# Announcing the closing branch of every tile loop in a four-layer graph network

## The reference

```python
x = _layernorm(x + _L0_gnn_ref(x, edge_index, ...))       # attention over edges, 8 heads, q.k logits, gelu
x = _layernorm(x + _L1_gnn_ref(x, src, dst, edge_type, edge_weight1, bases, w_comp))   # 32 relations of 8 bases
x = _layernorm(x + _L2_gnn_ref(x, src, dst, ...))         # two graph attention layers, 8 heads and 1 head
x = _layernorm(x + _L3_gnn_ref(x, edge_index, ...))       # attention, a state-space scan over sorted nodes, feed-forward
```

## Time and profile before

| | us |
|---|---|
| median of 3 runs | 10471.25 |
| lowest and highest run | 10463.4, 10483.5 |
| the profiled execution | 10561.48 |
| its span, first to last instruction | 10559.3 |
| slot build and first products, about 640 to 1060 | 420 |
| conv, 1060 to 2900 | 1840 |
| relation layer, 2900 to 4545 | 1645 |
| gat1 and gat2, 4545 to 7700 | 3155 |
| last layer, 7700 to 10020 | 2320 |
| join, 10020 to the end | 539 |

### The profile page before, as it was taken

How to read it: one execution, slowest core, us unless ns; L and a number is a source line. 1 busy time by engine, 2 the same in 40 slices (tenths; PEclk the granted TensorE clock), 3 DMA queues, 4 the chain that set the end, 5 groups by cost and what they waited for, 6 DMA issues and landing times. The chain is left out here.

```text
span 10559.3 us, 93192 instructions
## 1 busy us (share of the span) xinstructions
PE 3592.6 (34%) x15280; PEld 2794.6 (26%) x15281; DVE 5663.9 (54%) x11971; ACT 1229.9 (12%) x2744; POOL 5135.2 (49%) x4985
## 2 busy tenths in 40 slices
PE   3034343333255556611122200000034444444434
PEld 3011232222255556510111100000023333333323
DVE  8632666666521111157666656666655555555644
ACT  0001011111100001100000000000011222222211
POOL 0021555555465556656666556666544454444410
PEclk6556666666677778855555555555567666767666
DMA  0111444444222222223323222223222222222200
GB/s 19 51 42 27 120 128 121 120 128 122 77 76 73 65 66 81 67 58 80 80 76 82 60 64 76 75 74 80 62 68 69 78 79 68 76 73 70 60 28 7
DMA packets 485741, 772.46 MB, mean 73 GB/s; under 512 B 296031, under 2 KB 316310, under 8 KB 481979
## 3 DMA queue, kind: packets, MB, share of 16 engines
q0 software_dynamic: 265504, 666.90, 22.9%
q10 hardware_dynamic: 19838, 70.21, 1.8%
q1 hardware_dynamic: 200345, 34.81, 1.8%
HBM read 822.37 MB, written 46.03 MB: 82 GB/s over the span
## 5 line engine op out<-in xcount | busy, mean ns | idle before, releaser
L782 POOL DMA_INDIRECT gat_rows<-scratch_gat,gat_index x1856 | 1861.3, 1003 | 1050.0 <-issue 606.6
L1644 POOL DMA_INDIRECT m_rows<-scratch_gat,m_index x928 | 1064.4, 1147 | 1228.6 <-DVE m_work L1933 893.0
L782 POOL DMA_INDIRECT conv_rows<-scratch_kv,conv_index x928 | 931.4, 1004 | 796.3 <-DVE conv_work L861 363.7
L1211 POOL DMA_INDIRECT rel_rows<-scratch_x,rel_index x928 | 926.5, 998 | 612.5 <-issue 409.3
L1067 PE MATMUL conv_ps<-conv_work,k_ident 128*128 128x256 f32 x1856 | 672.2, 540 | 1275.0 <-DVE conv_work L861 1078.5
L1067 PEld LDWEIGHTS conv_ps<-conv_work,k_ident 128*128 128x128 f32 x1856 | 514.2, 284 | 1433.5 <-DVE conv_work L861 1111.8
L552 PE MATMUL gat_ps<-k_ident,gat_cur 128*128 128x128 f32 x100 | 34.4, 448 | 2350.1 <-issue 1029.4
L871 DVE TENSOR_REDUCE gat_red<-gat_work 128x256 f32<-128x2048 f32 x232 | 832.5, 3589 | 0.0
L1697 PE MATMUL m_ps<-m_work,k_ident 128*128 128x256 f32 x1664 | 556.9, 510 | 702.8 <-DVE m_work L1933 643.6
L1697 PEld LDWEIGHTS m_ps<-m_work,k_ident 128*128 128x128 f32 x1664 | 433.2, 266 | 824.2 <-issue 735.6
L552 PEld LDWEIGHTS gat_ps<-k_ident,gat_cur 128*128 128x128 f32 x100 | 14.5, 204 | 2385.3 <-issue 1045.3
(11 more groups left out here) (449 smaller groups left out, 7916.9 us busy)
## 6 DMA issues: line engine op xcount, KB each, us to landing
m_bc<-scratch_bc ACTq DMA_DIRECT2D x25, 2048.0 KB
gat_rows<-scratch_gat,gat_index POOLq DMA_INDIRECT x1856
conv_rows<-scratch_kv,conv_index POOLq DMA_INDIRECT x928
rel_rows<-scratch_x,rel_index POOLq DMA_INDIRECT x928
m_rows<-scratch_gat,m_index POOLq DMA_INDIRECT x928
scratch_runs<-e_runs_sb SPq DMA_DIRECT2D x1, 12890.6 KB
scratch_kv<-p_row ACTq DMA_DIRECT2D x25, 256.0 KB
gat_index<-scratch_slots SPq DMA_DIRECT2D x232, 4.0 KB
```

The source lines that it names most:

```text
L782: pool.indirect_dma_start(out=rows[b][:, s, :], out_offset=None, in_=table, in_offset=bass.IndirectOffsetOnAxis(ap=index[b][:, s:s + 1], a ...
L1211: pool.indirect_dma_start(out=rows[b][:, g, :], out_offset=None, in_=dr["x1"], in_offset=bass.IndirectOffsetOnAxis(ap=index[b][:, g:g + 1] ...
L1644: pool.indirect_dma_start(out=rows[b][:, s, :], out_offset=None, in_=dr["gat3"], in_offset=bass.IndirectOffsetOnAxis(ap=index[b][:, s:s + ...
```

## The change

A helper `tile_loop` is added, and every loop over tiles, on all five engines and in all stages that have one, is opened with it in place of `eng.Fori`; SP's loop over records in the relation layer too. The inner loops over chunks stay as they are.

```diff
+def tile_loop(nc, eng, first, end):
+
+    return nc.Fori(first, end, engines=(eng.engine,), hint_back_edge=True)
...
-            with v.Fori(0, T) as t:
+            with tile_loop(nc, v, 0, T) as t:
...
-            with sp.Fori(0, T) as t:
+            with tile_loop(nc, sp, 0, T) as t:
                 visit(sp, kp, t, load_record)
...
-            with pool.Fori(1, T) as t:
+            with tile_loop(nc, pool, 1, T) as t:
                 visit(pool, kp, t, gather)
...
-            with sp.Fori(1, last + 1) as r:
+            with tile_loop(nc, sp, 1, last + 1) as r:
                 sp.wait_ge(record_taken, r)
...
-            with eng.Fori(0, T - 2) as t:
+            with tile_loop(nc, eng, 0, T - 2) as t:
                 tile(t, True, True)
...
-            with v.Fori(0, T // B) as i:
+            with tile_loop(nc, v, 0, T // B) as i:
                 st = Steps(v, sems["steps"], BEFORE + i * PER)
```

More of the change, by code:

```diff
@@ L476, in _ @@
             nc.gpsimd.iota(slot_i[:], [[1, RUN]], base=0, channel_multiplier=0).then_inc(sems["zero"], 1)
-            with pool.Fori(0, T) as t:
+            with tile_loop(nc, pool, 0, T) as t:
                 lo, hi = bounds(pool, kp, t)
@@ L506, in _ @@
             pe.wait_ge(sems["loaded"], 16 * LOADS)
-            with pe.Fori(0, T) as t:
+            with tile_loop(nc, pe, 0, T) as t:
                 for k in range(2):
@@ L529, in _ @@
             act.wait_ge(sems["loaded"], 16 * LOADS)
-            with act.Fori(0, T) as t:
+            with tile_loop(nc, act, 0, T) as t:
                 for k in range(2):
@@ L988, in _ @@
             tile(0, True)
-            with v.Fori(1, T) as t:
+            with tile_loop(nc, v, 1, T) as t:
                 tile(t, False)
@@ L1050, in _ @@
             visit(act, kp, 0, exp)
-            with act.Fori(1, T) as t:
+            with tile_loop(nc, act, 1, T) as t:
                 visit(act, kp, t, exp, first_pair(t - 1))
@@ L1097, in _ @@
                 visit(pe, kp, 0, sum_slots)
-                with pe.Fori(1, T) as t:
+                with tile_loop(nc, pe, 1, T) as t:
                     visit(pe, kp, t, sum_slots, first_pair(t - 1))
@@ L2012, in _ @@
             tile(0, True, True, None)
-            with v.Fori(1, T - 2) as t:
+            with tile_loop(nc, v, 1, T - 2) as t:
                 tile(t, True, True, t - 1)
@@ L2073, in _ @@
             prime(pool, dr, spare, sems["written"])
-            with pool.Fori(0, T // B) as i:
+            with tile_loop(nc, pool, 0, T // B) as i:
                 pool.wait_ge(sems["out_ready"], i + 1)
@@ L2096, in turn @@
                 ins.then_inc(sems["turned"], 1)
-            with pe.Fori(0, T // B) as i:
+            with tile_loop(nc, pe, 0, T // B) as i:
                 pe.wait_ge(sems["turn"], i * 3 + 1)
@@ L2143, in take_root @@
                 act.activation(root[:], var[:], ACT.Sqrt).then_inc(sems["root"], 1)
-            with act.Fori(0, T // B) as i:
+            with tile_loop(nc, act, 0, T // B) as i:
                 act.wait_ge(sems["elu_in"], i + 1)
```

## The result

The changed kernel took 10490.32 us (median of 12 runs, 10453.28 to 10505.58), the kernel before beside it 10464.51 us (12 runs, 10439.14 to 10483.5): a ratio of 1.0019, 95% interval 1.0010 to 1.0028. By the ratio that is 20 us more, 10 to 29 by the interval; the two medians stand 26 us apart. The profiled execution of the changed kernel had a span of 10503.8 us in a run of 10505.58; that of the kernel before had been 10559.3 us, in a run of 10561.48. So the two profiled executions stand the other way round than the medians. From here on totals are compared by medians, and only parts by traces.

What follows compares the result with a forecast made beforehand. No engine was taken as the bound; tile heads stand in the chain. Nothing saved, 15 us of added instructions, two thirds showing as 10 us on the 10471.25 us median: 10481 us, range 10440 to 10525.

Steps and rivals of the forecast that it cites:

- the 0.2%: Whole kernel: about 0.2% (21 us) is what a measurement can tell from no change; chance of landing within it 0.67.
- What bounds the kernel: All tile loops: no engine is busy even 55% of the span; the head of a tile stands in the chain.
- Saved term nought: Back edges of all tile loops: none fetches code, so the announcement saves 0 us.
- The fifth rival: DVE's last-layer and PE's relation-layer bodies fetch after all, at most 97 us hidden: 10384 us, chance 0.02.
- Price of the instruction: Tile heads: 0.1 us per announcement (0.02 to 0.3), 148 times, 15 us; ends 3 and 44 us.
- The third rival: Closing branch: the announcement removes the gap to the next instruction, 148 x 0.25 = 37 us back: 10444 us, chance 0.06.
- What covers it: Tile heads: engines not added up, part given back from buffers ahead, two thirds of 15 us shows: 10 us.
- The second rival: Long tile heads: one more 0.7 us sequencer step in 33 heads, 23 us besides the 15: 10509 us, chance 0.10.
- The fetching rival: Tile heads: each announcement fetches its target although present, 148 x 2.1 = 311 us: 10782 us, chance 0.08.

Runs made afterwards that it cites:

- e9_sem8_again: Eight semaphore additions on which nobody waits at every tile head on every engine, no announcement, against the kernel before: 10774.44 us, ratio 1.0204.
- e3_hint8_dve: Eight announcements and a register move at each tile head on DVE alone, none on other engines, against the kernel before: 9237.75 us, ratio 1.0082.
- e4_hint8_rest: Eight announcements and a register move at tile heads on POOL, SP, ACT and PE, none on DVE, against the kernel before: 9178.75 us, ratio 1.0019.
- e5_hint1_all: The changed kernel unaltered, once more beside the kernel before on a chip with long steps: 10603.04 us, ratio 1.0039.
- e8_four_loads_hint: Four value loads per tile head in place of six, plus one announcement on every engine, against the kernel before: 10481.82 us, ratio 0.9918.
- e7_four_loads: Four value loads per tile head in place of six, the other two values summed, no announcement, against the kernel before: 10452.38 us, ratio 0.9893.
- e10_sem8_hint: Eight semaphore additions at every tile head plus one announcement on every engine, against the kernel before: 10844.71 us, ratio 1.0271.
- e12_three_loads: Three value loads per tile head in place of six, with one more schedule row, no announcement, against the kernel before: 10414.13 us, ratio 0.9862.
- e2_nop8_all: Eight no-operations intended, but only one register move added at nearly every tile head on all engines, no announcement, against the kernel before: 9167.62 us, ratio 1.0009.
- the first four runs: Eight announcements on all engines, on DVE alone, on the others alone, and one register move; the kernel before took 9160.75 us on their chip.
- e11_sem7: Seven semaphore additions at every tile head on every engine, no announcement, against the kernel before: 10735.72 us, ratio 1.0167.

## Why the prediction was right, and where its steps were off

**The total.** 20 us slower was measured (10 to 29; 26 by the medians), 10 were forecast, on a base that agrees (10464.51 against 10471.25). The ratio of 1.0019 lies inside the 0.2%, so it came out as forecast, but near the edge, and on a second chip the same kernel was 0.39% slower, outside it. The sign held both times; the size measured was twice and four times the forecast's. On the chip without long steps an announcement comes to 11 us (89/8), almost the 10 of the forecast, but that is partly luck. The price of 0.1 us was too high for it (0.065 to 0.07), and the two thirds that show, on one engine's head alone, were too low. The two errors cancel.

**What bounds the kernel: right.** That the tile's head is in the chain was the base of it all. Eight announcements and a move on DVE alone bring 77 of their 89 us; fewer value loads bring 109 and 151 us.

**Saved term nought: right.** No back edge fetches anything in the kernel before, and no fetch was saved: the stretch without instruction packets stays so. The fifth rival, that the longest bodies fetch after all, was wrong for this placement of the code. What it speaks of happens all the same. With the body starting 40 instructions further on and eight longer (e9_sem8_again), q14 moved five 8 KB packets per iteration (85 in 17) and DVE's back edge took 4 us; no run shows why there and not before. The forecast rested on a margin that it had not measured. And that an announced branch has nothing to save where nothing is fetched was the author's assumption, which no run shows; at the branch itself the runs showed some 0.05 us saved (next paragraph).

**Price of the instruction: a third too high on DVE.** It was 0.1 us by the nearest row; measured are 0.06 in the slot build, 0.065 from eight of them, and 0.08 from an announcement's start to the next instruction's (median of 148 in the changed kernel). Part of it comes back: by the records' own starts the gap from branch to next instruction went from 0.33 us to 0.28 in the last layer. The third rival, a cheaper branch, had bet on 0.25; it is 0.05. The forecast's saving of nought leaves these 0.05 us out.

**What covers it: the step that failed.** "I take two thirds as showing: 10 us" and "I don't add the five engines up" were both wrong. By e3_hint8_dve and e4_hint8_rest DVE's part shows almost in full (77 of 89 us) and the others' comes on top (18 us). On a chip without long steps that still makes no more than 11 us; the term that was missing is what comes on top on a chip with long steps, 9 to 30 us. The second rival had such a term (23 us). The objection against it, that the first instructions of a long head are short, holds for DVE (none of its 148 announcements took over 0.5 us, and one in e5_hint1_all) but not for two others. The announcements of POOL and SP in the edge layers of the changed kernel:

```profile
L805 POOLq BRANCH_PREFETCH_HINT  x72: 17/44/710, 1158.0 to 7573.6; - x72
```

```profile
L767 SPq BRANCH_PREFETCH_HINT  x75: 3/691/709, 1056.5 to 7541.2; - x75
```

On SP the median announcement took 691 ns; on POOL up to 710, and 30 of its 151 over 500 ns, which is some 20 us. On SP it is 59 of 189, some 41 us. What of that reaches the end wasn't tried alone, so that POOL and SP as the place of the missing term are argued and not shown. Plain instructions come to 27 us for one at every head on such chips. The announcement itself showed 20, 41, 29 (e8_four_loads_hint less e7_four_loads) and 70 us (e10_sem8_hint less e9_sem8_again), each with an interval of 10 to 30 us to either side. Whether it is dearer than a plain instruction there stays open.

**The fetching rival: out.** It had 0.08 and 10782 us. Eight announcements on five engines moved no packet more.

## What to carry to other kernels

Announce a loop's branch where the trace shows instruction packets inside the loop, and measure even then: here the fetching of 4 us per iteration was gone with it and nothing was won, it seems because the head met more long steps in its place (7.9 in a mean head of the last layer against 6.1). Without such packets it is one more instruction at the head of a tile, where 77 of the 89 us of DVE's showed (e3_hint8_dve), and each such instruction at 148 heads costs 11 us on one chip and 20 to 41 us on others, and 70 us in one kernel (e10_sem8_hint). The same reading points to the better change: in such a head it is the value loads with their range tests, 0.7 us each (4.2 us for six), that are worth taking out: 109 us for two (e7_four_loads), 151 us for three (e12_three_loads).

## What the runs showed of the hardware

**Two kinds of chip.** The kernel before takes 9160.75 us on one chip and 10464.51 to 10565.45 us on the others, 14 to 15% more (granted clock of PE over the span 0.651 in e2_nop8_all, 0.632 in the first profile). The difference is in the stages that gather rows alone: by DVE's first operations the slot build and the join take 390 and 506 us in e2_nop8_all and 391 and 507 in the first profile, the last layer 2030 and 2349. On the chip of the first four runs, two of the costliest groups (line, operation, count, busy us, mean ns) were

```profile
L802 POOL DMA_INDIRECT gat_rows<-scratch_gat,gat_index x1856 | 1858.1, 1001 | 618.9 <-issue 561.9
...
L891 DVE TENSOR_REDUCE gat_red<-gat_work 128x256 f32<-128x2048 f32 x232 | 832.4, 3588 | 0.0
```

and in the first profile

```profile
L782 POOL DMA_INDIRECT gat_rows<-scratch_gat,gat_index x1856 | 1861.3, 1003 | 1050.0 <-issue 606.6
...
L871 DVE TENSOR_REDUCE gat_red<-gat_work 128x256 f32<-128x2048 f32 x232 | 832.5, 3589 | 0.0
```

1001 against 1003 ns and 3588 against 3589. (Not all groups are that close: PE is busy 3533.6 and 3592.6 us in all.) What stands out are sequencer steps of 0.7 us in the place of 0.02 to 0.3: 885 of 14479 on DVE in the first profile are over 0.5 us, 27 of 14627 in e2_nop8_all. That they make up the whole of the difference isn't shown. The difference is no product of profiling, since the unprofiled runs have it too. The long steps come on several engines at a time: of SP's steps that start within 1.5 us of the start of a long step of DVE 44% are long, against 18% over the whole run. They also come with the row gathers: in the loops of the gathering stages, slices of 2 us in which DVE starts a long step have 71 to 120 packets of the gathers' queue in the mean, the others 32 to 81. That is a coincidence in time; its cause wasn't tried and stays open.

**An announced branch.** The announcement takes 39 ns on DVE (median of the 72 at L994), and from the branch to the next instruction it is 0.28 us with it and 0.33 without (last layer, changed kernel and kernel before). With it the refetching of a body that lay past the edge was gone, 85 packets and 3.5 to 4.3 us per back edge against none and 0.3 us (e9_sem8_again, e10_sem8_hint).

**An edge of six instructions.** The body at instructions 2342 to 2619 of DVE's program is kept (e11_sem7); the one at 2347 to 2625 is fetched in each iteration, 85 packets in 1650 us (e9_sem8_again).
